# Expert stage of a transformer block: another order of shared and routed units, uneven streams, weight staging by DMA, and silu

## The reference

```
x = x + layernorm(attention(layernorm(x)))    # 16 heads of 8 channels, elu+1, rotary embedding, softmax, depthwise conv of v
x = x + layernorm(experts(layernorm(x)))

logits = xt @ gate_w.T;  scores = softmax(logits);  idx = top_2(scores + gate_b)    # 8 experts, 2 per token
cw = one_hot(idx) weighted by scores
h1 = xt @ w1[e].T + b1[e];  h3 = xt @ w3[e].T + b3[e]      # 128 -> 256 (128 pairs g, l)
a = swiglu(h1 * h3)         # g = min(g, 7), l = clip(l, -7, 7);  g * sigmoid(1.702 g) * (l + 1)
routed = sum over e of cw[e] * (a @ w2[e].T + b2[e])
out = routed + the same MLP with shared weights sw1, sw3, sw2, applied to every token
```

## Time and profile before

| what | value |
|---|---|
| median of three runs | 1421.89 us (1420.94 to 1422.09) |
| profiled execution, its own time | 1411.95 us |
| its span, first to last instruction | 1409.8 us |
| busy: TensorE, DVE, ScalarE, GpSimd | 1194.9, 1134.7, 938.4, 842.3 us |
| mean granted clock of TensorE, as a share of 2.4 GHz | 0.901 |
| end of attention | 977.2 us |
| routed units (first to last hidden product) | 993.0 to 1218.6 us |
| shared units (same) | 1219.5 to 1380.1 us |

### The profile page before, as it was taken

One profiled execution on the slowest core, in us unless ns is written; L12 is line 12 of the kernel. 1 busy time (PEld: TensorE's weight loads), 2 busy tenths in 40 slices (PEclk: granted clock), 3 DMA queues, 4 the chain that ended last, 5 costly groups with the idle time before them and its releaser, 6 DMA issues. The chain is left out here.

```text
span 1409.8 us, 22726 instructions
## 1 busy us (share of the span) xinstructions
PE 1194.9 (85%) x6712; PEld 514.4 (36%) x6712; DVE 1134.7 (80%) x2581; ACT 938.4 (67%) x1743; POOL 842.3 (60%) x1112
## 2 busy tenths in 40 slices
PE   1699999999999998998998998961898988888885
PEld 0122222222222222232232222221676766666553
DVE  1589999999989998999999999534677789866666
ACT  1038888887786785886887887851787777643332
POOL 5244465564675775875776765544686465533575
PEclk9559999999999998999999999985899999987665
DMA  2362232232232241241332331200345444412222
GB/s 69 74 183 60 55 88 71 66 82 70 72 94 74 72 111 51 82 112 42 89 88 56 92 86 47 80 32 28 99 134 171 139 138 138 132 45 57 70 71 81
DMA packets 103956, 119.89 MB, mean 85 GB/s; under 512 B 13189, under 2 KB 80910, under 8 KB 103566
## 3 DMA queue, kind: packets, MB, share of 16 engines
q1 hardware_dynamic: 93728, 97.55, 24.8%
q0 software_dynamic: 8192, 16.79, 4.3%
q10 hardware_dynamic: 1914, 4.10, 0.8%
HBM read 58.89 MB, written 59.51 MB: 84 GB/s over the span
## 5 line engine op out<-in xcount | busy, mean ns | idle before, releaser
L923 DVE TENSOR_REDUCE MX<-psS 128x1 f32<-128x512 f32 x1024 | 653.8, 681 | 68.3 <-PE psS L417 60.4
L672 ACT ACTIVATE PR<-psST 128x512 f32<-128x512 f32 x986 | 536.9, 599 | 160.7 <-PE psST L405 148.0
L417 PE MATMUL psS<-KS,QS 48*128 48x512 bf16 x1024 | 366.7, 405 | 52.5 <-DVE MX L923 28.5
L405 PE MATMUL psST<-QS,KS 51*128 51x512 bf16 x986 | 336.5, 391 | 22.6 <-ACT PR L672 8.0
L431 PE MATMUL psPV<-PR,V 128*32 128x512 f32 x2048 | 279.6, 618 | 7.9 <-ACT OT L586 2.7
L405 PEld LDWEIGHTS psST<-QS,KS 51*128 51x128 bf16 x986 | 76.4, 93 | 379.2 <-ACT PR L672 328.1
L1695 POOL DMA_INDIRECT GOT<-scratch_y,FROM x128 | 132.5, 1035 | 61.5 <-issue 31.3
L417 PEld LDWEIGHTS psS<-KS,QS 48*128 48x128 bf16 x1024 | 84.4, 94 | 115.8 <-DVE MX L923 89.8
L1024 POOL DMA_INDIRECT scratch_x<-XN,POSI x96 | 95.6, 995 | 27.8 <-issue 27.2
L1051 POOL TENSOR_TENSOR ROT<-ROT,RES 128x512 f32<-128x512 f32 x32 | 40.5, 1268 | 88.9 <-DVE RES L731 88.9
L1327 PE MATMUL psH<-XH,WS 128*128 128x512 f32 x184 | 81.4, 443 | 0.0
(11 more groups left out here) (173 smaller groups left out, 2200.0 us busy)
## 6 DMA issues: line engine op xcount, KB each, us to landing
scratch_parts<-PT SPq DMA_DIRECT2D x192, 128.0 KB
QS<-scratch_parts SPq DMA_DIRECT2D x64, 192.0 KB, 3.4
KS<-scratch_parts SPq DMA_DIRECT2D x64, 192.0 KB, 4.4
XR<-scratch_x SPq DMA_DIRECT2D x46, 256.0 KB
scratch_y<-YR SPq DMA_DIRECT2D x46, 256.0 KB
scratch_x<-ZERO SPq DMA_DIRECT2D x18, 256.0 KB, 2.1
X<-in_x SPq DMA_DIRECT2D x16, 256.0 KB, 4.8
scratch_turned<-XT SPq DMA_DIRECT2D x16, 256.0 KB, 4.4
```

What stands on the lines that cost most here:

```text
L405: nc.tensor.matmul(bank(st_banks(t), k)[:], KS[t.par][rows, h // 2, kc * P:(kc + 1) * P], QS[t.par][rows, h // 2, :], start=True, stop=Tru ...
L417: nc.tensor.matmul(bank(psS, k)[:], QS[b.par][rows, h // 2, qc * P:(qc + 1) * P], KS[b.par][rows, h // 2, :], start=True, stop=True).then_ ...
L672: nc.scalar.activation(PR[:, s % 2, j, :], bank(st_banks(t), k)[:], ACT.Exp, scale=SCALE).then_inc(st_exp, 1)
L923: nc.vector.tensor_reduce(out=MX[:, qc, h:h + 1], in_=bank(psS, k)[:], axis=AX.X, op=ALU.max).then_inc(s_max, 1)
```

## The change

- **Order.** Four shared units come first, then the routed units of stream 0, then those of stream 1 with a shared unit after every third, then the six that are left. Slots are numbered p; `ORDER[p]` says what is in a slot. There are 62 as before.
- **Streams.** Stream 0 has ten batches and 27 units, stream 1 six batches and 19 units. Their tables are computed apart (`unit_tables`, in eleven steps): the first in attention's iteration 15, the second in slots 4 to 14.
- **Staging.** WS and DS are filled by two DMAs from WALL and WD on SP's queue, two slots ahead (`stage` of SP), in place of ScalarE's and GpSimd's copies.
- **swiglu.** ScalarE computes silu(1.702 g) in one step (SG), HA = (L + 1) x SG; the down weights are scaled by 1 / 1.702, not by 0.5. GT is gone.
- **Gates.** All CW are transposed at once at the start, 16 transposes of 128x128, into CWT. The b2 term of a shared unit is one 128x512 product with a block-diagonal BD.
- **Batch ends.** A shared unit's psY goes to R(b) on ScalarE (`evict`); `weigh` adds both gathered rows to it in eight steps; ACC and the separate Z are gone. Gathers run four to a slot, the ends of batches follow at slots FINISH[b]: 37 to 55 in steps of two for batches 0 to 9, 62 to 72 for the rest. GOT has three buffers.
- **WALL.** The shared pair is split first, the eight others in slots 0 to 2.
- **Attention.** In iteration 16 the scatters of batch 11 come after the residual, not before; the zero rows of stream 0 are written in iteration 16, not 14. `load_weights` has four DMAs for BD.

```diff
-WEIGHTS = 4
+WEIGHTS = 7
...
-SPAN = B // STREAMS
+SPAN = 10
...
-UNITS = SPAN * N * TOPK // TILE + NE - 1
+UNITS = tuple(n * N * TOPK // TILE + NE - 1 for n in (SPAN, B - SPAN))
+FIRST_UNIT = (0, UNITS[0])
+MOST_UNITS = max(UNITS)
+STEPS = SPAN * N // TILE
...
+                        if t.c == SPAN + 5 and j == 3 and 3 <= s <= 3 + TABLE_WAITS:
+                            table(dve, 0, s - 2)
...
-                if out.live and out.c < B - 4:
+                if out.live and out.c < B - 4 and t.c < B:
...
+                if out.live and out.c < B - 4 and t.c >= B:
+                    scatter(out, 0)
+                    scatter(out, 1)
...
+        FRONT = 4
+        PACE = 4
+
+        ORDER = [("S", b) for b in range(FRONT)] + [("R", i) for i in range(UNITS[0])]
+        shared = iter(range(FRONT, B))
+        for i in range(UNITS[1]):
+            ORDER.append(("R", UNITS[0] + i))
+            if i % 3 == 2:
+                ORDER.append(("S", next(shared)))
+        ORDER += [("S", b) for b in shared]
+        ALL = len(ORDER)
+        ROUTED = sum(UNITS)
+        SLOT_R = [ORDER.index(("R", i)) for i in range(ROUTED)]
+        SLOT_S = [ORDER.index(("S", b)) for b in range(B)]
+        LAST = [SLOT_R[UNITS[0] - 1], SLOT_R[ROUTED - 1]]
+        GATHER_AT = [slot + LAG + 2 for slot in LAST]
+        FIRST_B = [0, SPAN]
+        FINISH = [GATHER_AT[int(b >= SPAN)] + (GATHERS * (b - FIRST_B[int(b >= SPAN)] + 1)) // PACE + 1 for b in range(B)]
+        END = max(FINISH) + 6
...
+            def stage(i):
+                if i == 0:
+                    sp.wait_ge(split, EXP_ALL)
+                    sp.wait_ge(halved, 1)
+                if i in FIRST_UNIT:
+                    sp.wait_ge(expert_ready, FIRST_UNIT.index(i) + 1)
+                if i >= D_BUFS:
+                    sp.wait_ge(y_psum, SLOT_R[i - D_BUFS] + 1)
+                    sp.wait_ge(gl_ready, 2 * (SLOT_R[i - D_BUFS] + 1))
+                if i >= W_BUFS:
+                    sp.wait_ge(h3_psum, 2 * (SLOT_R[i - W_BUFS] + 1))
+                e = sp.value_load(EXPERT[0:1, i:i + 1], min_val=0, max_val=NE)
+                sp.dma_start(WS[:, i % W_BUFS].rearrange("p a m g f -> p (a m g f)").bitcast(F32),
+                             WALL[:, bass.ds(e, 1)].rearrange("p e a m g f -> p (e a m g f)").bitcast(F32)
+                             ).then_inc(staged[i % D_BUFS], 16)
+                sp.dma_start(DS[:, i % D_BUFS], WD[:, bass.ds(e, 1)].rearrange("p e c -> p (e c)")
+                             ).then_inc(staged[i % D_BUFS], 16)
...
+            for p in range(3):
+                load(p)
+            for p in range(END):
+                if p == SLOT_R[UNITS[0]] - 6:
                     zero_tails()
+                if routed(p - LAG):
+                    store_rows(p - LAG)
+                if routed(p + 2):
+                    stage(ORDER[p + 2][1])
+                load(p + 3)
+                if p - 6 in FINISH:
+                    store_out(FINISH.index(p - 6))
+            store_out(B - 1)
...
+            def turn_gates():
+                for g in range(QC):
+                    for b in range(QC * g, QC * (g + 1)):
+                        last = nc.tensor.transpose(psH[g][:, b % QC * P:(b % QC + 1) * P],
+                                                   CW[:, QC * b:QC * (b + 1), :].rearrange("p q e -> p (q e)"), IDF[:])
+                    last.then_inc(cw_psum, 1)
...
+            def down(p):
+                pe.wait_ge(ha_ready, p + 1)
+                if due(p):
+                    pe.wait_ge(y_evicted, p)
+                if not routed(p):
+                    nc.tensor.matmul(psY[:], CWT[:, ORDER[p][1], :], BD[:].rearrange("p q c -> p (q c)"),
+                                     start=True, stop=False)
                 for q in range(QC):
+                    last = nc.tensor.matmul(psY[:, q * P:(q + 1) * P], HA[:, p % HA_BUFS, q * P:(q + 1) * P],
+                                            down_rows(p)[:, 0:C], start=routed(p), stop=routed(p) or q == QC - 1)
                 last.then_inc(y_psum, 1)
...
-            def tanh(u):
-                wait_clip(act, u, 0)
-                if due(u - 1):
-                    act.wait_ge(gate_done, u - 1)
-                nc.scalar.activation(TH[:, u % 2, :], G[:, u % 2, :], ACT.Tanh, scale=ALPHA / 2).then_inc(tanh_done, 1)
+            def silu(p):
+                wait_clip(act, p, 0)
+                if due(p - 1):
+                    act.wait_ge(ha_ready, p - 1)
+                nc.scalar.activation(SG[:, p % 2, :], G[:, p % 2, :], ACT.Silu, scale=ALPHA).then_inc(silu_done, 1)
+            def evict(p):
+                act.wait_ge(y_psum, p + 1)
+                i = ORDER[p][1]
+                if routed(p):
+                    if i >= 2:
+                        act.wait_ge(y_stored[i % 2], 16 * (i // 2))
+                    place = YR[:, i % 2]
+                else:
+                    if i < R_BUFS:
+                        act.wait_ge(split, min(2 * (i % QC) + 3, EXP_ALL))
+                    else:
+                        act.wait_ge(x2_ready, i - R_BUFS + 1)
+                    place = R(i)
+                nc.scalar.activation(place, psY[:].rearrange("p (q c) -> p q c", q=QC), ACT.Copy).then_inc(y_evicted, 1)
...
+            weights_high(NE)
             turn(0)
+            for g in range(QC):
+                turned_gates(g)
+            for p in range(END):
+                turn(p + 1)
+                if p < ALL:
+                    hidden(p, 0)
+                if 0 <= p - 1 < ALL:
+                    silu(p - 1)
+                if 0 <= p - LAG < ALL:
+                    evict(p - LAG)
+                if p < ALL:
+                    hidden(p, 1)
+                if p < NE // 3 + 1:
+                    for e in range(3 * p, min(3 * p + 3, NE)):
+                        weights_high(e)
+                if p - 3 in FINISH:
+                    scale(FINISH.index(p - 3))
...
-            def gated(u):
-                dve.wait_ge(tanh_done, u + 1)
-                if u >= 2:
-                    dve.wait_ge(ha_ready, u - 1)
-                nc.vector.scalar_tensor_tensor(out=GT[:, u % 2, :], in0=TH[:, u % 2, :], scalar=1.0, in1=G[:, u % 2, :],
...
+                dve.wait_ge(y_evicted, SLOT_S[b] + 1)
+                for k in range(TOPK):
+                    for q in range(QC):
+                        last = nc.vector.scalar_tensor_tensor(
+                            out=R(b)[:, q, :], in0=GOT[:, b % G_BUFS, k, q, :],
+                            scalar=WSEL[:, k, b * QC + q:b * QC + q + 1], in1=R(b)[:, q, :], op0=ALU.mult, op1=ALU.add)
+                    if k == 0:
+                        last.then_inc(weighted, 1)
+                        dve.wait_ge(weighted, b + 1)
+                last.then_inc(r_ready, 1)
...
-            def combine(b):
-                dve.wait_ge(y_psum, ROUTED + b + 1)
-                dve.wait_ge(r_ready, b + 1)
-                if b >= 2:
-                    dve.wait_ge(z_ready, b - 1)
-                nc.vector.tensor_tensor(ACC[:, b % 2], psY[:].rearrange("p (q c) -> p q c", q=QC), R(b),
...
+                for st in range(STREAMS):
+                    for n in range(PACE * (p - GATHER_AT[st]), PACE * (p - GATHER_AT[st] + 1)):
+                        if 0 <= n < (SPAN, B - SPAN)[st] * GATHERS:
+                            gather(FIRST_B[st] * GATHERS + n)
+                if p - 2 in FINISH:
+                    rsqrt(FINISH.index(p - 2))
```

More of the change, by code:

```diff
@@ L568, in _ @@
                              (GB[:], gate_b.unsqueeze(0).to_broadcast([P, NE])),
-                             (TAB[:], table.to_broadcast([P, sum(TABLE.values())])),
+                             (TAB[:], numbers.to_broadcast([P, sum(TABLE.values())])),
                              (COUNT[:].bitcast(U16), count),
@@ L1406, in stage @@
[L1406 to L1416 removed]
+                    nc.scalar.activation(XH[:, p % 2, :], XTL[:, b % 2, :], ACT.Copy).then_inc(xh_ready, 1)
```

634 lines of the change are left out of this document (269 added, 365 removed).

## The result

The changed kernel takes 1438.74 us (median of 4, 1433.98 to 1446.22) against 1421.41 of the kernel before in the same session: ratio 1.0145, 95% interval 1.0073 to 1.0216. It is slower by 1.5%. The forecast was 1369 us, range 1350 to 1400. The profiled execution took 1443.0 us, span 1441.2, so the sum to compare with is the forecast's span of 1357: it is 84 us short.

A forecast was written before the change was run, and what follows sets the result against it. Room was seen in the tail of some 190 us, where 16 shared units and eight gather batches stand behind routed units. Stage times summed to a 1357 us span, plus 2.15, times 1.0070: 1369 us, range 1350 to 1400.

The forecast's parts named there:

- The sum: Whole kernel: the terms added up to 1357 us of span, 1369 us of time; chance 0.60, own range 1350 to 1385.
- Start of the experts: Expert stage start: four shared units go first once the shared WALL pair is split; first routed unit at 1005 us.
- the 1 us at the end of attention: End of attention: batch 11's scatters moved behind X let the last XN start earlier; gain 1 us, bounds 0 and 2.
- Routed units: Slots 4 to 30: SP's queue, from store to XR issue to transposes, sets a period of 4.6 us; 27 units, 124 us.
- Rival B: Transfers or SP's queue come late, but the change still gains: period 5.4 us, 1385 to 1410; chance 0.20.
- Rival C: The on-chip weight copy is slow and the kernel slower: gain lost at 6.3 us a unit, 1455 at 7; chance 0.07.
- Zero rows: SP's eight zero transfers, now ahead of a weight copy too, hold back XR and idle TensorE: 7 us.
- Slots 34 to 55: GpSimd's 80 gathers and batch ends take 115 us, 5.9 us a slot; batch 9 done at 1270 us.
- The tail: After the last routed store at 1279: six batches, 48 gathers, 66 us, to 1345, then 12.6 us to the end.
- D: No gain because TensorE's clock falls: at half clock a unit takes 8.4 us, +48 us, 1417; chance 0.07.
- E: Silu needs its own function table each time: two loads a slot on ScalarE, +32 us, 1401; chance 0.02.
- the staging copies themselves bring little: Within the sum: moving WS and DS copies to DMA gains little; the gain is in mixing shared and routed units.

The follow-up runs named there:

- after_again: The changed kernel without an edit, on a chip where the kernel before takes 1402 us: 1391.7 us, ratio 0.9918 to the kernel before.
- engines_stage: The changed kernel with staging taken back: ScalarE copies WS and GpSimd copies DS, in the same slots; 1380.0 us, ratio 0.9728 to the kernel before.
- load_first: The changed kernel with the load of XR issued ahead of the two staging transfers on SyncE's queue; 1373.8 us, ratio 0.9805 to the kernel before.
- before_dma_stage: The kernel before, with WS and DS staged by two transfers between store and load on SyncE's queue, engine copies gone; 1472.2 us, ratio 1.0374.
- gap2_b: The changed kernel with a GpSimd memset of 128x512 behind every second gather; 1424.5 us, ratio 1.0057 to the kernel before.
- tie_gathers: The changed kernel, GpSimd waiting in each slot from 34 on for DVE's first gate product before its gathers; 1422.5 us, ratio 1.0032.

## Why the prediction was wrong

The sum was 84 us short. Two steps failed: the issues on SyncE's queue between store and load were sized too small, and the gathers were counted as GpSimd's time alone. Where the distance to the forecast arises (us; forecast of HA: 1013 for slot 4, then 4.6 a slot, 7 for the zero rows, 2.5 for the row tables):

| up to | forecast | result | late | late on kind 2 (after_again) |
|---|---|---|---|---|
| HA of slot 4 | 1013 | 1018.5 | 5.5 | 3.5 |
| HA of slot 25 | 1109.6 | 1129.1 | 19.5 | 15.5 |
| HA of slot 26 | 1121.2 | 1144.3 | 23.1 | 19.1 |
| HA of slot 33 | 1155.9 | 1178.2 | 22.3 | 19.1 |
| store of slot 55 | 1279 | 1349.7 | 70.7 | 29.8 |
| end | 1357 | 1441.2 | 84.2 | 36.0 |

- *Start of the experts.* WALL began at 980.0, not 976. With the same attention code it began at 976 to 979 in the traces of kind 2 and at 979 to 992 in those of kind 1, so the 1 us at the end of attention can't be seen. Silu's single load of tables: right.
- *"Routed units": the step that failed first.* I put 3.5 + 2.5 + 3.1 = 9.1 us on two slots; it is 3.58 + 3.63 + 3.05 = 10.26 where the chain runs undisturbed. The mechanism was right, and one term mis-sized: store to load, 3.63 for 2.5. The issues of WS and DS take 0.51 us each (assumed 0.35), and from the issue of DS to that of XR it is 1.86 us (assumed 1.11): I took the register read from rows where no transfer stood ahead of it, and behind the two transfers it takes 0.85 us, not 0.27. 21 slots by 0.67: +14 us. Rival B's reason ("all behind one eviction") named the place. Against engines_stage (4.24) the staging costs 1.03 us a slot there, and the copies that it replaces cost nothing in these slots: ScalarE's 1.06 us were in idle time, as the rows had shown.
- *The copy itself.* Not slow: from 1018 to 1129 us q1 moves 22.73 MB at a share of 59.6%, 344 GB/s against 325 in the earlier trace rows. Rival C is out. The Trainium skill, "DMA: Bandwidth & Descriptors", Anatomy of one DMA, made WS an estimate of 3.2 us; load_first's median of 3.0 agrees. The page gives its fit for transfers that GpSimd issues, and here SyncE issues them.
- *Zero rows.* 7 us forecast, 10.6 measured (15.23 less 4.6); the eight issues take 8.01 us (8.34 before), but the load behind them has two stagings ahead.
- *Slots 34 to 55: the step that cost most.* From the HA of slot 33 to the store of slot 55 the result takes 171.5 us, forecast 123.1. Slots 33 and 34 take 32.9 us and not 11.8, 21 us more; slots 37 to 55 take 6.91 us, not 5.9: +18; the remaining 9 lie where I joined the two regimes. No rival had this: nothing in my text made a run of gathers cost anything to an engine other than GpSimd. I had counted 80 gathers as GpSimd's own time, and the new pacing lets 24 of them stand in one run (three buffers of GOT, no copy of DS between). On kind 2, without late signals, these slots take 5.85 us and slots 33 and 34 take 12.4: there the period was right, and only the join is 10.7 us off.
- *The tail.* From the store of slot 55 to the end 78 us forecast, 91.5 measured, 84.2 on kind 2. The 7 us between the kinds fit the second run of 24 gathers with its wait of 15.7 us, but no run takes that one away alone.
- *Rivals.* B had the right cause of the first failure at the right price (1385 to 1410); the changed kernel takes 1391.7 on kind 2, which lies inside the stated range, though by B and not by the sum, and gains 0.8% there where the sum had 3.7%. The sign on kind 1 came from what B didn't hold. D: the clock is 0.89 in slots 37 to 55, and 0.90 on kind 2 without loss; not a cause. It is 0.70 in slots 33 to 35, where TensorE stands idle, and follows the stall. E's price doesn't fit the sum, which gives ScalarE 2.8 us a slot and not 3.3: two loads would have added some 22 us, not 32; one load was seen. The statement "the staging copies themselves bring little" was too kind: on kind 1 taking them back is worth 4.2%, in part through the gathers that they break up, which makes a loss of 1.5% a gain of 2.7%.

Shown by runs: what staging by transfers costs, with the longer runs of gathers that come with it (engines_stage, before_dma_stage), that part of it is the place ahead of the load (load_first), that unbroken runs of gathers go with the late signals, on kind 1 alone (gap2_b, tie_gathers, after_again). Not shown: how much of the 4.2% is the queue alone on kind 1 in slots 33 to 55 (the first 31 us are). Open: why a run of gathers does so, whether TensorE's work or only its signal is late (its records stand at their usual pace, and the first reads of psY, psH and psX behind the stall follow within 2.5 us of each other at 1206 to 1209), why the register read is three times as long behind two transfers, and what differs between the chips or the sessions.

## What to carry to other kernels

Before work is moved from an engine to a DMA queue, follow the queue: a transfer is free in bandwidth long before it is free in order, and what is issued behind an eviction is late by every issue and register read in front of it. An engine's copy in its idle time is cheaper than that, and idle is to be read from the stage in question: the copies cost nothing in slots 4 to 25 and half a microsecond a slot in 37 to 55. Take the cost of an issue or a register read from rows in which the same instructions stand ahead of it. Don't let GpSimd issue long runs of indirect gathers beside TensorE's work: put its other work between them; and measure a change on more than one chip before its sign is believed, since this one was 1.5% slower on one and 0.8% faster on another.

## What the runs showed of the hardware that was not expected

- On three of the five chips (and in the result's session), ScalarE and DVE wait for TensorE up to 18.4 us with no work on record at the end of the wait while GpSimd issues indirect gathers back to back (0.94 us and 0.30 of issue each); in the result's trace an eviction starts 22 us after the recorded end of its products and 2 us after the last gather. Eight indirect scatters in a row do it too (a wait of 8.1 us). A memset of 0.55 us behind every second gather takes the sum from over 105 us to 3.4. Plain transfers of rows of the same size from GpSimd don't do it. On two chips it wasn't seen.
- SyncE's register read ahead of the load of XR takes 0.27 us at the median in the kernel before and in engines_stage, 0.85 us behind two transfers on the same queue (0.84 in before_dma_stage), more than an issue.
- A copy of 512 KB from SBUF to SBUF with register-given source lands 3.0 us after its issue, among other traffic.
